# Loading and quantizing ternary weights inside the preceding attention stage of an eight-stage transformer kernel

## The reference, cut to what matters

```python
# layer 1, feed-forward ("think"): a vector per sequence goes through 4 steps of a small MLP,
# is multiplied with a gate of every token, and the sum is normed
out = x + jax.nn.sigmoid(x @ gate_w + gate_b) * broadcast
# layer 2 (the third layer), attention: 16 heads over 64 keys with compressed q and k, rope,
# a window mask, softmax, read-out, output projection
# layer 2, feed-forward (ternary): three weight matrices, each 704 x 256 or 256 x 704
def _quantize(w):
    gamma = jnp.mean(jnp.abs(w))
    return jnp.clip(jnp.round(w / (gamma + EPS)), -1.0, 1.0)
hidden = jax.nn.sigmoid(x @ _quantize(w1).T) * (x @ _quantize(w2).T)
out = hidden @ _quantize(w3).T
# layers 0 and 3, feed-forward: experts
h = jax.nn.silu(tokens @ w1) * (tokens @ w3)
```

## Time and profile before

| | us |
|---|---|
| median of 3 runs | 2742.14 (2735.84 to 2747.07) |
| the profiled execution | 2754.47 |
| its span | 2752.7 |
| PE busy | 2011.5 (73%) |
| DVE busy | 1745.9 (63%) |
| POOL busy | 1170.6 (43%) |
| ACT busy | 967.1 (35%) |

### The profile page before, as it was taken

How to read it: one execution, slowest core, us unless ns; L and a number is a source line. 1 busy time by engine, 2 the same in 40 slices (tenths; PEclk the granted TensorE clock), 3 DMA queues, 4 the chain that set the end, 5 groups by cost and what they waited for, 6 DMA issues and landing times. The chain is left out here.

```text
span 2752.7 us, 48931 instructions
## 1 busy us (share of the span) xinstructions
PE 2011.5 (73%) x17042; PEld 1511.4 (55%) x17074; DVE 1745.9 (63%) x3743; ACT 967.1 (35%) x2509; POOL 1170.6 (43%) x1482
## 2 busy tenths in 40 slices
PE   4776927536976077777777479959999999458995
PEld 3666826315855066666666356635666665135774
DVE  5554479324554878888888544457887885633446
ACT  2442201102423233333343122215666666222331
POOL 2430000462323745555555222335887887063331
PEclk9777965657988589999999789978999999778998
DMA  4224100561076100000000000024444441222336
GB/s 116 55 54 162 38 8 2 161 163 47 5 183 106 31 1 0 0 0 0 0 0 0 32 1 1 1 49 97 104 110 111 96 112 45 71 90 66 107 105 212
DMA packets 142050, 174.97 MB, mean 64 GB/s; under 512 B 30380, under 2 KB 123740, under 8 KB 137116
## 3 DMA queue, kind: packets, MB, share of 16 engines
q1 hardware_dynamic: 132044, 150.51, 20.7%
q0 software_dynamic: 9808, 21.93, 2.6%
HBM read 113.01 MB, written 58.79 MB: 62 GB/s over the span
## 5 line engine op out<-in xcount | busy, mean ns | idle before, releaser
L2512 DVE TENSOR_REDUCE mx<-bank 128x2 f32<-128x512 f32 x512 | 321.2, 680 | 91.4 <-PE bank L2374 91.3
L2478 ACT ACTIVATE e<-bank 128x512 f32<-128x512 f32 x512 | 269.1, 606 | 137.3 <-PE bank L2394 137.2
L2306 POOL TENSOR_TENSOR es<-e 128x256 f32<-128x256 f32 x384 | 271.0, 728 | 92.7 <-ACT e L2478 92.2
L2374 PE MATMUL bank<-k,q 72*128 72x256 bf16 x1024 | 203.7, 284 | 34.8 <-DMA k<-k_parts 34.8
L1667 POOL TENSOR_TENSOR q_l<-q_l,rot_l 64x1024 f32<-64x1024 f32 x64 | 150.5, 2352 | 182.0 <-DVE rot_l L1811 182.0
L2394 PE MATMUL bank<-q,k 74*128 74x256 bf16 x1024 | 195.5, 274 | 7.2 <-DMA q<-rows 4.7
L1708 PE MATMUL bank<-wvo,rd_l 128*128 128x256 f32 x512 | 120.6, 389 | 37.2 <-ACT rd_l L1766 37.2
L2374 PEld LDWEIGHTS bank<-k,q 72*128 72x128 bf16 x1024 | 92.1, 100 | 95.8 <-issue 51.6
L2411 PE MATMUL bank<-e,val 128*32 128x256 f32 x2048 | 140.5, 392 | 3.1 <-ACT nd L2473 0.6
L1686 PE MATMUL bank<-qcT,wq_abs 96*128 96x128 f32 x1024 | 125.0, 281 | 11.2 <-ACT qcT L1736 11.2
L1708 PEld LDWEIGHTS bank<-wvo,rd_l 128*128 128x128 f32 x512 | 95.7, 192 | 62.4 <-ACT rd_l L1766 50.4
(11 more groups left out here) (455 smaller groups left out, 5308.2 us busy)
## 6 DMA issues: line engine op xcount, KB each, us to landing
q<-q_parts SPq DMA_DIRECT2D x32, 576.0 KB
k<-k_parts SPq DMA_DIRECT2D x96, 192.0 KB
got<-rows SPq DMA_DIRECT2D x71, 128.5 KB
rows<-no_row SPq DMA_DIRECT2D x1, 9088.0 KB, 43.9
moe_rows<-zero_b SPq DMA_DIRECT2D x16, 512.0 KB, 5.8
w<-in_e0w SPq DMA_DIRECT2D x16, 512.0 KB
moe_in<-moe_rows SPq DMA_DIRECT2D x16, 512.0 KB, 8.8
parts_y<-y SPq DMA_DIRECT2D x32, 256.0 KB, 4.6
```

What stands on the lines that cost most here:

```text
L2306: nc.gpsimd.tensor_tensor(es[:, n, :], e[:, n, 0, :], e[:, n, 1, :], ALU.add).then_inc(s["sum_ready"], 1)
L2374: last = nc.tensor.matmul(scores(r)[:, qt * D:(qt + 1) * D], q[0:R, b, h * D + qt * P:h * D + qt * P + P], k[0:R, b, h * D:(h + 1) * D], s ...
L2478: nc.scalar.activation(e[:, slot(i, r), :, :].rearrange("p k n -> p (k n)"), scoresT(r)[:, :], ACT.Exp).then_inc(s["exp_ready"], 1)
L2512: v.tensor_reduce(mx[:, a.n, 0, at:at + 2], scores(r)[:, :].rearrange("p (a n) -> p a n", a=2), AX.X, ALU.max, negate=True).then_inc(s["ma ...
```

## The change

**Ternary weights.** The first block of the ternary stage is gone. Its loads are issued by SP at the start of the third layer's attention, into the space that held the raw weights of that stage. The work on DVE lies between the steps: the three sums of magnitudes in front of step 12, the scale behind step 13 (with the matmul of ones on PE, behind the scores of tile 14), and the three quantizing operations of each matrix in 8 pieces of 176 or 192 columns, behind the steps 14 to 29: one piece behind every even step, two behind every odd one. The loops of DVE, PE and POOL are split in two for it. The quantized matrices lie in buffers that are held through all earlier stages.

**Think stage.** The seven loads of weights become ten, issued singly or in pairs between the loads of the groups 1 to 6. Some small buffers of the stage move into the space of the raw weights.

**Experts.** ACT computes `Silu` instead of `Sigmoid`, and the first of the two products on DVE, with the wait behind it, is gone.

The diff, cut to its core:

```diff
@@ experts of layer 0 (those of layer 3 alike) @@
-nc.scalar.activation(sig[:, g % 2, :], gates(g)[:, 0:F0], ACT.Sigmoid).then_inc(s["sig_ready"], 1)
+nc.scalar.activation(sig[:, g % 2, :], gates(g)[:, 0:F0], ACT.Silu).then_inc(s["sig_ready"], 1)
...
-v.tensor_tensor(sig[:, g % 2, :], gates(g)[:, 0:F0], sig[:, g % 2, :], ALU.mult).then_inc(s["e_chain"], 1)
-dve.wait_ge(s["e_chain"], g + 1)
@@ think stage, SP @@
+quarter = lambda n: slice(4 * n, 4 * n + 4)
+ahead = [[], [(wuqT, c.d["wuqT"])], [(wukT, c.d["wukT"])], [(wqr, c.d["wqr"]), (c.seg_i[:, :], c.d["seg"])],
+         [(wuvT, c.d["wuvT"]), (c.wdq[:, :, :], c.d["wdq"].rearrange("(k p) n -> p k n", p=P))],
+         [(wo[:, quarter(0), :], c.d["wo2"][:, quarter(0), :]), (wo[:, quarter(1), :], c.d["wo2"][:, quarter(1), :])],
+         [(wo[:, quarter(2), :], c.d["wo2"][:, quarter(2), :]), (wo[:, quarter(3), :], c.d["wo2"][:, quarter(3), :])]]
...
-    if g == TH - 1:
-        for dst, src in ((wuqT, c.d["wuqT"]), (wukT, c.d["wukT"]), (wqr, c.d["wqr"]), (wuvT, c.d["wuvT"]),
-                         (wo, c.d["wo2"]), (c.wdq[:, :, :], c.d["wdq"].rearrange("(k p) n -> p k n", p=P)),
-                         (c.seg_i[:, :], c.d["seg"])):
-            sp.dma_start(dst, src).then_inc(s["l_weights"], 16)
+    for dst, src in ahead[g] if g < len(ahead) else ():
+        sp.dma_start(dst, src).then_inc(s["l_weights"], 16)
@@ attention of the third layer @@
+FIRST_RUN = 7
+RUNS = NT // 2 - 1
+PIECES = RUNS - FIRST_RUN
...
+def total():                                   # PE, between the two loops
+    pe.wait_ge(s["q_zero"], 2)
+    pe.wait_ge(s["q_sums"], 3)
+    nc.tensor.matmul(bank(0, 3)[:, 0:3], ones, abs_sums[:, :], start=True, stop=True).then_inc(s["q_total"], 1)
+    pe.wait_ge(s["q_seen"], 1)
...
+def scales():
+    dve.wait_ge(s["q_total"], 1)
+    v.tensor_scalar(inv[:, :], bank(0, 3)[:, 0:3], 1.0 / (HID2 * D), EPS2, ALU.mult, ALU.add).then_inc(s["q_seen"], 1)
+    dve.wait_ge(s["q_seen"], 1)
+    qch.link(v.reciprocal(inv[:, :], inv[:, :]))
+def quantize(n, i):
...
+    ch.link(v.tensor_scalar(below[:, 0:w], src[:, at], inv[:, n:n + 1], -0.5, ALU.mult, ALU.is_lt))
+    ch.link(v.tensor_scalar(src[:, at], src[:, at], inv[:, n:n + 1], 0.5, ALU.mult, ALU.is_gt))
+    ch.link(v.tensor_tensor(dst[:, at], src[:, at], below[:, 0:w], ALU.subtract))
...
-with dve.Fori(0, NT // 2 - 1) as i:
+with dve.Fori(0, FIRST_RUN - 1) as i:
     step(2 * i, 0)
     step(2 * i + 1, 1)
+magnitudes()
+step(2 * FIRST_RUN - 2, 0)
+step(2 * FIRST_RUN - 1, 1)
+scales()
+with dve.Fori(FIRST_RUN, RUNS) as i:
+    step(2 * i, 0)
+    quantize(0, i)
+    step(2 * i + 1, 1)
+    quantize(1, i)
+    quantize(2, i)
@@ ternary stage @@
-        with ExitStack() as pre:
...
-                            last = nc.tensor.matmul(dst, lhsT, w12[:, k, n, hidden], start=(k == 0 and part == 0),
+                            last = nc.tensor.matmul(dst, lhsT, w12[:, n, HID2 * k + hidden.start:HID2 * k + hidden.stop], start=(k == 0 and part == 0),
```

More of the change, by code:

```diff
@@ L39 @@
 HID2, EPS2 = 704, 1e-8
+FT2 = -(-HID2 // P)
 H3 = 8
@@ L1262, in stage_l1_think @@
         row = {n: first.take(M, 1, D)[:, 0, :] for n in ("in_gamma", "in_beta", "agg_b", "pn_gamma", "pn_beta", "d2_b", "bc_b")}
+        last_x, n1, th = (first.take(M, 1, D)[:, 0, :] for _ in range(3))
+        nT = first.take(P, 1, DK * M)[:, 0, :]; hT = first.take(P, FT, M)
         then = Carve(c.raw)
@@ L1605, in stage_l2_attention, with run, pair @@
                       "nope_copied rope_done rope_added kv_ready key_ready scores_ready max_ready shifted_ready exp_ready sum_ready prob_ready turned_ready "
-                      "turned_copied read_ready read_copied out_ready x_done drop_chain masked summed add_chain")
+                      "turned_copied read_ready read_copied out_ready x_done drop_chain masked summed add_chain q_loaded q_zero q_sums q_total q_seen q_chain")
+        FIRST_RUN = 7
+        RUNS = NT // 2 - 1
+        PIECES = RUNS - FIRST_RUN
+        quant = Carve(c.raw)
+        raw12 = quant.take(P, 2, DK * HID2); raw3 = quant.take(P, FT2, D); ones = quant.take(P, 1, P)[:, 0, :]
+        below = quant.take(P, 1, FT2 * D // PIECES)[:, 0, :]
+        abs_sums = sb("abs_sums", [P, 3]); inv = sb("inv_q", [P, 3])
         def bank(j, n): return c.bank[4 * j + n]
         block = ctx.enter_context(nc.Block())
[L1611 to L1616, removed]
+        def run(eng, ahead, behind, after=lambda t, j: None, between=None):
+            def pair(i):
                 for j in range(2):
@@ L1620, in run @@
                     after(2 * i + j + 1, 1 - j)
+            ahead(0, 0)
+            after(0, 0)
+            with eng.Fori(0, FIRST_RUN) as i:
+                pair(i)
+            if between:
+                between()
+            with eng.Fori(FIRST_RUN, RUNS) as i:
+                pair(i)
             ahead(NT - 1, 1)
@@ L1631, in heads, with _ @@
             return slice(n * HP, n * HP + HP)
+        @block.sync
+        def _(sp):
+            for n, name in enumerate(("t1", "t2")):
+                sp.dma_start(raw12[:, n, :].rearrange("p (k n) -> p k n", k=DK),
+                             c.d[name].rearrange("(k p) n -> p k n", p=P)).then_inc(s["q_loaded"], 16)
+            full = HID2 // P
+            sp.dma_start(raw3[:, 0:full, :], c.d["t3"][0:full * P, :].rearrange("(k p) n -> p k n", p=P)).then_inc(s["q_loaded"], 16)
+            sp.wait_ge(s["q_zero"], 1)
+            sp.dma_start(raw3[0:HID2 - full * P, full, :], c.d["t3"][full * P:HID2, :]).then_inc(s["q_loaded"], 16)
+            sp.wait_ge(s["q_loaded"], 64)
         @block.gpsimd
@@ L1639, in _ @@
             nc.gpsimd.memset(kv2[:, :, :, :], 0.0).then_inc(s["l_zero"], 1)
+            nc.gpsimd.memset(raw3[:, FT2 - 1, :], 0.0).then_inc(s["q_zero"], 1)
+            nc.gpsimd.memset(ones, 1.0).then_inc(s["q_zero"], 1)
             flat = lambda ap: ap.rearrange("p h n -> p (h n)")
@@ L1724, in scores @@
                         last.then_inc(s["scores_ready"], 1)
-            run(pe, front, back, scores)
+            def total():
[3 more added lines that the diff above has]
+                pe.wait_ge(s["q_seen"], 1)
+            run(pe, front, back, scores, total)
         @block.scalar
@@ L1854, in _ @@
             back(NT - 1, 1)
-FT2 = -(-HID2 // P)
 def stage_l2_ternary(nc, c):
@@ L1869, in stage_l2_ternary @@
         hrest = sb("hrest_t", [P, LANES, HW]); hlow = sb("hlow_t", [P, LANES, HW], BF16)
[L1870 removed]
+        s = open_sems(nc, ctx, "pad_set xn_ready feat_ready feat_copied rest_ready "
                       "low_ready up_ready sig_ready h_ready turned_ready hT_ready hrest_ready hlow_ready down_ready "
                       "x_done add_chain")
[L1873 to L1922 removed]
@@ L2900, in sigmoid @@
                 wait(act, "hid_ready", u - 1)
-                nc.scalar.activation(sig[:, u % 2, :], gates(u)[:, 0:HID3], ACT.Sigmoid).then_inc(s["sig_ready"], 1)
+                nc.scalar.activation(sig[:, u % 2, :], gates(u)[:, 0:HID3], ACT.Silu).then_inc(s["sig_ready"], 1)
             def copy(u):
@@ L2986, in layers, with first_layers @@
 def layers(nc, c):
+    with ExitStack() as tern:
+        c.w12 = tern.enter_context(nc.sbuf_tensor("w12", [P, 2, DK * HID2], BF16))
+        c.w3 = tern.enter_context(nc.sbuf_tensor("w3q", [P, FT2, D], BF16))
+        first_layers(nc, c)
+        finish_stats(nc, c, "st5")
+        stage_l2_ternary(nc, c)
+    last_layer(nc, c)
+def first_layers(nc, c):
     with ExitStack() as keys:
```

55 lines of the change are left out of this document (19 added, 36 removed).

## The result

The changed kernel takes 2779.44 us (median of 4 runs, 2777.78 to 2785.36) against 2744.61 (2735.84 to 2749.53): ratio 1.0127, 95% interval 1.0094 to 1.016. It is 35 us slower. I had forecast 2740 with a range of 2726 to 2755: the time lies outside, and it went the other way.

The account below looks back on a forecast made before the run. Stages between barriers, with DVE's ring of work and waits setting the third layer's attention. Terms -27.6 + 31.5 + 3.9 + 2.4 - 11.2 - 1.2 = -2.2 us took the profiled 2754.5 to 2752.3; 12.3 lower for the median, 2740.0; range 2726 to 2755.

Parts of the forecast that it names:

- part 1: Ternary stage: its first block goes, so the second block's norm starts earlier, -27.6 us.
- part 2: Third layer's attention: quantizing pieces in DVE's ring cost 1.0 per even seam, 2.9 per odd, +31.5 us over eight turns.
- held: Attention seams: a DVE operation is stopped until POOL's rope_add ends; 1.0 us in an even seam, without it 0.2.
- rival B: Attention, odd seams: PE's pause reaching 3.6 lets its clock fall to 0.50, +16 us, 2756 us; chance 0.15.
- part 3: Attention: magnitudes ahead of step 12 cost +3.9 us, the scale behind the matmul of ones +2.4 us.
- TensorE's slack of 1.0: Attention seam: PE can take a norm later by 1.0 us; taken off the 4.9 us of the magnitudes.
- part 4: Think stage: group 2's loads land earlier with only wuqT ahead, removing POOL's wait, -11.2 us.
- Rival C: Think stage: group 2's load comes no sooner, POOL still waits 6 us, 2746 us; chance 0.1.
- part 5: Experts: a product less per unit, -1.2 us at layer 3's end; two table loads at about 2.66 us would give +5.3.
- Rival A: Attention: pieces aren't held while POOL runs and fit into waiting time, 1.0 us less per seam, 2724 us; chance 0.2.

Follow-up runs that it names:

- tail_pieces: Changed kernel with no pieces between the steps, the three matrices quantized whole behind the last step: 2725.3 us, 0.9923 against the kernel before.
- one_piece: Changed kernel with a piece behind even steps only, the other two matrices quantized whole behind the last step: 2735.12 us, 0.9961 against the kernel before.
- tern_fill: Changed kernel with the earlier think stage and experts, plus dummy TensorE matmuls in the second loop's seams: 2768.37 us, 1.0093 against the kernel before.
- before_fill: Kernel before with the same dummy matmuls (5 and 10 in turn) behind the scores in all loop steps: 2792.47 us, 1.0175.
- pool_static: Changed kernel with magnitudes on ScalarE, scales behind the maxima of step 12, pieces on GpSimd: 2697.1 us, 0.9824 against the kernel before.
- silu_only: Kernel before with only Silu in place of Sigmoid and one product less in the experts: 2746.11 us, 1.0002.

## Why the prediction was wrong

- **The ternary block (part 1): right.** -27.6 forecast, -28.0 by the stage, of which 11 are the quantizing itself (tail_pieces has that behind the attention, 1556.25 to 1567.39).
- **The pieces, directly (part 2): right in the sum, with some luck.** The working gave +1.3 and +2.9 for the norm's end, less the waits that a later VectorE doesn't meet, 3.9 a turn. Measured: +1.52 and +3.3 at the norm; 1.26 for a step with one piece (one_piece and tern_fill), 2.98 with two (tern_fill alone, so with the dummy work), 4.2 a turn and 33 us in all against 31.5. The odd seam came near by two errors that cancel in part: I took its first operation as not held, but it is held like the even one's, 1.23 in place of 0.31, +0.92; and its gaps together grew by 0.70 where I had taken 1.29. The 0.07 that I read as one gap in the ternary block were two.
- **The step that failed: TensorE's clock was left out of the sum and made rival B, at 0.15.** I gave it the odd seams only, from the point where the pause reaches 3.6, with 2.0 us a turn: +16. The runs show +30 in the loop (changed kernel against tern_fill). The odd seam's pause never reached 3.6, or the 3.4 that I had worked out: the second half of the scores lies between a pause of 1.21 and one of 2.40. The clock fell even so, and in some even seams too, behind 0.53, together with the 1.2 that had always been there. That the loop stayed at 1.00 with its own pauses, on which both the sum and B's threshold rest, said nothing of how near it was to falling; the argument that I gave against B, work of the other lane, didn't keep the clock up. one_piece shows how near: 1.3 us more in every second step let it fall in every fourth. What exactly makes it fall is not shown: no run finds a single pause that decides. And the loss isn't only the odd seam's: a lower clock stretches the projection (6.35 for 3.84), and VectorE waits up to 3.6 us for it.
- **Magnitudes and scales (part 3): both too low**, 3.9 and 2.4 against 5.7 and 5.3. For the magnitudes the norm ends 3.9 later, as forecast, if not for my reason: TensorE's slack of 1.0 gives nothing back, since the next maxima wait for VectorE itself, but the idle time behind the statistics is 0.56 shorter and the norm is no longer stretched. The other 1.8 come behind it, with a lower clock that I had left out here too: behind a pause of 2.97 it is at 0.50 from 1194.8 to 1201.6, the projection takes 5.92, and VectorE waits 2.45 for it. For the scales I had priced two passages, but not that TensorE comes to the matmul of ones only at 1233.63, behind the second half of the scores, and VectorE stands idle for 3.84 us:

```profile
1231.98 1.72 PE L1750 MATMUL bank<-key_l,q_l 128*64 128x64 f32 x32 [1.19 <-POOL q_l L1696]
1233.63 0.59 PE L1758 MATMUL bank<-abs_sums,raw_weights 128*128 128x3 f32 x2
1234.26 0.16 DVE L1889 TENSOR_SCALAR inv_q<-bank 128x3 f32<-128x3 f32 x1 [3.84 <-PE bank L1758]
...
1238.33 5.84 PE L1715 MATMUL bank<-qcT,wq_abs 96*128 96x128 f32 x32 [0.35 <-ACT qcT L1771]
```

```profile
1232.40:1242.50 10.10, 7.85 (x53) 6.90 (x50) 5.84 (x14) 1.89 (x4) 3.58 (x5) 0.50 0.01 2
```

  The norm ends 3.4 later by that; the other 1.9 of the 5.3 come behind it, where the clock is at 0.50 and the projection takes 5.84. The clock had fallen at 1232.3, before TensorE had waited for anything new in this seam, and behind pauses that the kernel before has too (1.16, 0.54 and 1.19 us; before, 1.16, 0.39 and 1.20). Two steps earlier it had fallen behind the magnitudes. Why it fell here is open.

- **Think stage (part 4): right**, -11.2 forecast, -11.5 measured by itself (interval -8 to -16), and 11.1 us less of POOL's wait; by the length of the stage it is 8 to 10. That it came out to 0.3 us is in part luck. Rival C is out: the landing wasn't held up by the one matrix ahead of it.
- **Experts (part 5): nothing**, 0 against -1.2, inside what can be told.
- **Rival A is out**: no piece found room under POOL's addition; the first of each of the 16 seams took 1.21 to 1.24 us and ended 0.11 behind it.

The sum with what was measured: -28.0 + 33.2 + 30.3 + 5.7 + 5.3 - 9.9 = +36.6, against +35 of the medians. Of the 39 us between this sum and the forecast's -2.2, the clock in the loop is 30.

## What to carry to other kernels

Work that is put into one engine's seam costs what it does to every engine behind it: before pricing a delay on a ring, ask how long TensorE will stand there and whether the loop's clock can bear it, since a loop that shows 1.00 everywhere may be just above the edge, as this one was. A small dose shows it: one piece in every second seam (one_piece) was enough. When work has to be hidden, put it on the engine that waits longest at that place, not on the one that is fastest at it: GpSimd took 1.6 to 2.8 times as long per operation and, with the magnitudes on ScalarE, all of it was hidden; the change went from +35 us to -44. Moving loads past each other, the smaller part of the change, was read from one row and came out within what the runs can tell.

## What the hardware showed that I had not expected

- Dummy matmuls can pay: in the seams of tern_fill 1.4 and 2.5 us of work without use took 16 to 21 us off the kernel (37 in the profiled executions), in before_fill the same work, in all steps of the attention, cost 50.
- The shortest fall of the clock seen, 3.4 us at 0.50, costs 0.97 us in its step (one_piece).
- The Trainium skill (SBUF — State Buffer, "SBUF: two separate sides") lets the port's holder keep it for a whole instruction. The traces agree for an operation with one tensor as input: 1.23 us in place of 0.31 for L1899 (a TENSOR_SCALAR of 176 columns) beside POOL's addition, ended 0.11 behind it. VectorE's rope products, which read one tensor from PSUM, kept their 0.69 while GpSimd ran 5.2 us of quantizing (pool_static).
- The two more loads of the function table that `Silu` wants took 1.28 us each (silu_only) and didn't show in the length of the stages. In both places the load begins 0.02 behind the copy before it; the first `Silu` starts 0.24 behind the load in the one, where it waits for TensorE, and 0.01 in the other. So of part 5's 2.66 us nothing beyond the 1.28 shows.
